# 32-head attention with its score operands in 48 partitions, two items' score products issued alternately

## What is computed

```python
q = layernorm(x)                       # (4, 256, 256): 32 heads of 8
k = v = ctx                            # (4, 256, 64):   8 heads of 8
# for each sequence b, group g, head h of the group:
scores = q[b, g, h] @ k[b, g].T * 8 ** -0.5      # 256 x 256
x[b, g, h] += softmax(scores) @ v[b, g]          # 256 x 8
```

## Time and profile before

| | |
|---|---|
| median of 3 runs | 812.61 us (811.94 to 814.03) |
| span of the profiled execution | 812.5 us |
| PE / DVE / ACT / POOL busy, whole span | 89% / 71% / 52% / 24% |
| the stage, first score product to last output | about 590 to 712 us |
| loop of 28 items at the full clock | 3.19 us an item |

### The profile page before, as it was taken

The page is one execution under the profiler, slowest core; times in us unless marked ns, Lnnn a source line. Parts: engine busy times, 40 slices in busy tenths (PEclk is TensorE's granted clock), DMA queues, the critical chain, the costliest instruction groups (busy, mean ns, idle before and its releaser), DMA issues. The chain is left out here.

```text
span 812.5 us, 13314 instructions
## 1 busy us (share of the span) xinstructions
PE 722.5 (89%) x4826; PEld 462.7 (57%) x4826; DVE 577.6 (71%) x1117; ACT 425.3 (52%) x888; POOL 198.0 (24%) x298
## 2 busy tenths in 40 slices
PE   5999989999999999999757469999589999879997
PEld 3555666666666666666533345666344444368886
DVE  5578678686767667686669854565668999665666
ACT  4557753544636364543649655455366676533332
POOL 2422010303123030303225314120121111352450
PEclk9999999999999999999979679999859999969999
DMA  4725422111202111110153006130010323403111
GB/s 120 194 60 158 148 70 69 48 45 34 76 7 72 30 49 36 42 43 1 27 135 75 9 8 191 45 80 2 21 41 21 81 59 90 120 2 106 54 50 52
DMA packets 49760, 52.24 MB, mean 64 GB/s; under 512 B 10116, under 2 KB 40388, under 8 KB 49588
## 3 DMA queue, kind: packets, MB, share of 16 engines
q1 hardware_dynamic: 49062, 51.06, 23.4%
q10 hardware_dynamic: 634, 0.33, 0.2%
HBM read 26.58 MB, written 2.04 MB: 35 GB/s over the span
## 5 line engine op out<-in xcount | busy, mean ns | idle before, releaser
L427 DVE TENSOR_REDUCE a_nm<-ps 128x2 f32<-128x512 f32 (+1 forms) x112 | 75.3, 688 | 28.4 <-PE ps L723 19.4
L2499 DVE TENSOR_REDUCE x_nm<-ps 128x2 f32<-128x512 f32 x128 | 84.9, 685 | 12.4 <-PE ps L2640 10.1
L2584 ACT ACTIVATE x_pt<-ps 128x1024 f32<-128x1024 f32 x64 | 62.4, 1020 | 34.6 <-PE ps L2668 33.9
L1535 PE MATMUL ps<-m_xp,m_mp 128*128 128x512 f32 x288 | 75.4, 397 | 1.0 <-DVE m_wr L1227 1.0
L1406 ACT ACTIVATE m_junk<-ps,m_nm 128x256 bf16<-128x256 f32 x128 | 58.6, 483 | 25.8 <-DVE m_nm L1244 25.8
L1191 POOL TENSOR_SCALAR fw<-fw,finv 128x256 f32<-128x256 f32 x24 | 11.6, 482 | 223.7 <-PE ps L1613 223.7
L2640 PE MATMUL ps<-kx,a_qs 96*128 96x256 bf16 x256 | 53.1, 296 | 8.2 <-DMA a_qs<-a_ks 6.5
L1535 PEld LDWEIGHTS ps<-m_xp,m_mp 128*128 128x128 f32 x288 | 50.7, 188 | 15.4 <-issue 6.1
L3068 PE MATMUL ps<-x_xp,x_wp 128*128 128x512 f32 x216 | 55.2, 407 | 0.0
L1207 DVE TENSOR_TENSOR m_qcs<-ps,mw_tab 64x512 f32<-64x512 f32 x64 | 44.0, 688 | 7.5 <-PE ps L1535 4.3
L1214 DVE TENSOR_TENSOR m_qcs<-ps,mw_tab 128x512 f32<-128x512 f32 x64 | 41.1, 684 | 7.4 <-PE ps L1535 7.1
(11 more groups left out here) (306 smaller groups left out, 1673.8 us busy)
## 6 DMA issues: line engine op xcount, KB each, us to landing
a_qs<-a_parts SPq DMA_DIRECT2D x48, 128.0 KB
a_ks<-a_parts SPq DMA_DIRECT2D x48, 128.0 KB
m_q<-m_qs SPq DMA_DIRECT2D x32, 128.0 KB
x_gb<-scr_g SPq DMA_DIRECT2D x8, 512.0 KB, 3.8
fw<-in_f_w SPq DMA_DIRECT2D x12, 256.0 KB
a_qs<-a_ks SPq DMA_DIRECT2D x48, 64.0 KB
mw_wq<-in_m_wq SPq DMA_DIRECT2D x8, 256.0 KB, 2.8
mw_wo<-in_m_wo SPq DMA_DIRECT2D x8, 256.0 KB, 2.8
```

Of the source, the lines that this page charges most:

```text
L427: dve.tensor_reduce(dst, src, AX.X, ALU.max, negate=True).then_inc(mx_done.sem, 1)
L1535: mm = pe.matmul(c.ps[:, QB_BANKS[k], :], mp[:, p % 2, w, dt, tile * P:(tile + 1) * P], xp[:, x, dt, half_cols(half)], start=((dt, w, x) = ...
L2499: dve.tensor_reduce(nm[:, n % ITEMS, QT * u:QT * u + QT], c.ps[:, u % 2, :].rearrange("p (t k) -> p t k", t=QT), AX.X, ALU.max, negate=Tru ...
L2584: act.activation(pt[:, n % 2, kt, :], c.ps[:, 2 + 2 * kt:4 + 2 * kt, :].rearrange("p b n -> p (b n)"), ACT.Exp, scale=SCALE).then_inc(exp_ ...
```

## The change

The zero rows are gone: S_ROWS is 48 and T_ROWS is 50. Items take turns at partitions 0 and 64 (even n at 0, odd n at 64), so that two items' operands lie in separate halves of the rows. The key tile is written twice, once for each half. A query transfer that read 128 partitions becomes two that read 64 each, one to each half; with the same memory the query tile holds six units and not three. `place` and the head layout of the normalised input are changed so that each half receives the right heads. On PE, each S of item n + 4 is issued around one T matmul of item n + 1: S first half, T matmul, S second half.

```diff
-    GROUPS, S_ROWS, T_ROWS, HD = 8, 96, 98, 8
+    GROUPS, S_ROWS, T_ROWS, HD = 8, 48, 50, 8
+    BASES = (0, 64)
...
-    def clear(self, sp):
-
-        sp.wait_ge(self.made.sem, 2)
-        some = slice(TERMS * self.HD, self.S_ROWS)
-        sp.dma_start(self.kx[some, :, :], self.zeros[some, :].unsqueeze(1)
-                     .broadcast_to([self.S_ROWS - TERMS * self.HD, self.GROUPS, TOK])).then_inc(self.sent.sem, 16)
...
     def send(self, sp):
+        for base in self.BASES:
+            sp.dma_start(self.kx[base + self.S_ROWS:base + self.T_ROWS, :, :],
+                         self.ones[0:2, :].unsqueeze(1).broadcast_to([2, self.GROUPS, TOK])).then_inc(self.sent.sem, 16)
...
-                    sp.dma_start(self.kx[term:TERMS * self.HD:TERMS, :, :], self.parts[:, part, :]).then_inc(self.sent.sem, 16)
-        sp.dma_start(self.kx[self.S_ROWS:self.T_ROWS, :, :],
-                     self.ones[0:2, :].unsqueeze(1).broadcast_to([2, self.GROUPS, TOK])).then_inc(self.sent.sem, 16)
-        sp.wait_ge(self.sent.sem, 16 * (TERMS + 2))
+                    for base in self.BASES:
+                        sp.dma_start(self.kx[base + term:base + self.S_ROWS:TERMS, :, :], self.parts[:, part, :])\
+                            .then_inc(self.sent.sem, 16)
+        sp.wait_ge(self.sent.sem, 16 * 2 * (TERMS + 1))
...
         def place(n):
 
-            return n // GROUPS, n % GROUPS
+            return n // GROUPS, n % GROUPS // 4 * 4 + (0, 2, 1, 3)[n % 4]
...
-        def queries(rows, n, h, count=1):
-            return qx[rows, n // 4 % RINGS, 4 * (n % 4) + h:4 * (n % 4) + h + count, :]
+        def own_rows(n, first, last):
+
+            return slice(BASES[n % 2] + first, BASES[n % 2] + last)
+
+        def queries(n, first, last, h, count=1):
+            at = n % 4 // 2 * 4 + h
+            return qx[own_rows(n, first, last), n // 4 % SLOTS_Q, at:at + count, :]
...
-                            sp.dma_start(qx[term:TERMS * HD:TERMS, k % RINGS, :, :], parts[:, dt, part, seq_cols(b)])\
-                                .then_inc(part_in[k].sem, 16)
+                            for s, base in enumerate(BASES):
+                                sp.dma_start(qx[base + term:base + S_ROWS:TERMS, k % SLOTS_Q, :, :],
+                                             parts[64 * s:64 * s + 64, dt, part, seq_cols(b)])\
+                                    .then_inc(part_in[k].sem, 16)
...
+                def side_by_side(n, u, n_t, kt, h):
+
+                    may_score(n, u)
+                    if h == 0:
+                        may_score_t(n_t, kt)
+                    score(n, u, 0)
+                    mm = score_t(n_t, kt, h)
+                    if h:
+                        mm.then_inc(st_done.sem, 1)
+                    score(n, u, 1).then_inc(s_done.sem, 1)
...
                 for n in range(N - LAG):
-                    scores(n + LAG, 0)
-                    scores_t(n + 1, 0)
-                    scores(n + LAG, 1)
+                    side_by_side(n + LAG, 0, n + 1, 0, 0)
+                    side_by_side(n + LAG, 1, n + 1, 0, 2)
                     product(n, 0)
                     max_transpose(n + TLAG)
-                    scores(n + LAG, 2)
+                    side_by_side(n + LAG, 2, n + 1, 1, 0)
                     product(n, 1)
-                    scores(n + LAG, 3)
-                    scores_t(n + 1, 1)
+                    side_by_side(n + LAG, 3, n + 1, 1, 2)
```

More of the change, by code:

```diff
@@ L1869, in _ @@
                         .then_inc(w_in, 16)
-                keys.clear(sp)
+                sp.wait_ge(keys.made.sem, 1)
                 alibi.moves(sp, keys)
@@ L2192, in open @@
         self.turnable = sb("ordered", [P, TT, CTX])
-        self.ones, self.zeros = sb("ones", [P, TOK], BF16), sb("zeros", [P, TOK], BF16)
+        self.ones = sb("ones", [P, TOK], BF16)
         self.full, self.rest, self.parts = sb("full", [CTX, TOK]), sb("rest", [CTX, TOK]), sb("parts", [CTX, 3, TOK], BF16)
@@ L2224, in constants @@
         pool.memset(self.ones[:, :], 1.0).then_inc(self.made.sem, 1)
-        pool.memset(self.zeros[:, :], 0.0).then_inc(self.made.sem, 1)
-    def clear(self, sp):
-        sp.wait_ge(self.made.sem, 2)
-        some = slice(TERMS * self.HD, self.S_ROWS)
-        sp.dma_start(self.kx[some, :, :], self.zeros[some, :].unsqueeze(1)
-                     .broadcast_to([self.S_ROWS - TERMS * self.HD, self.GROUPS, TOK])).then_inc(self.sent.sem, 16)
     def remainder(self, pool):
@@ L2265, in cross_attention @@
     N = BATCH * GROUPS
-    S_ROWS, T_ROWS = keys.S_ROWS, keys.T_ROWS
-    UNITS = N // 4
+    S_ROWS, T_ROWS, BASES = keys.S_ROWS, keys.T_ROWS, keys.BASES
+    UNITS, SLOTS_Q = N // 4, 2 * RINGS
+    SHARE = HEADS // 4
     LAG, TLAG = 4, 3
@@ L2296, in cross_attention @@
         dense = sb("dense", [DENSE_ROWS, BATCH - 1, 4, SEQ])
-        qx = c.qflat[:, :].rearrange("p (r h q) -> p r h q", r=RINGS, h=HEADS // 2)
+        qx = c.qflat[:, :].rearrange("p (r h q) -> p r h q", r=SLOTS_Q, h=SHARE)
         kx = keys.kx
@@ L2340, in head_inner @@
         def head_inner(t):
-            return c.xn[:, t, :].rearrange("p (a d h) -> p a h d", a=DT, d=HD)
+            return c.xn[:, t, :].rearrange("p (e d h) -> p e h d", d=HD, h=SHARE)
         def head_outer(t):
-            return c.x[:, t, :].rearrange("p (a h d) -> p a h d", a=DT, d=HD)
+            return c.x[:, t, :].rearrange("p (e h d) -> p e h d", d=HD, h=SHARE)
         def residual(s):
@@ L2369, in shift_rows @@
         def shift_rows(n):
-            return queries(slice(S_ROWS, T_ROWS), n, 0, 4)
+            return queries(n, S_ROWS, T_ROWS, 0, 4)
         with nc.Block() as block:
@@ L2416, in _ @@
                     if RINGS <= k < UNITS and step < 3:
-                        if step == 0:
-                            sp.wait_ge(st_done.sem, st_done.at(8 * (k - RINGS + 1)))
+                        if step == 0 and k >= SLOTS_Q:
+                            sp.wait_ge(st_done.sem, st_done.at(8 * (k - SLOTS_Q + 1)))
                         send(k, step, (hi_done, mid_done, lo_done)[step])
@@ L2629, in turn, with may_score, score, scores @@
                     mm.then_inc(xn_tr.sem, 1)
[L2631 to L2634, removed]
+                def may_score(n, u):
                     if u == 0 and n % 4 == 0:
-                        pe.wait_ge(part_in[n // 4].sem, part_in[n // 4].at(16 * TERMS))
+                        pe.wait_ge(part_in[n // 4].sem, part_in[n // 4].at(16 * 2 * TERMS))
                     if n > 0 or u > 1:
                         pe.wait_ge(mx_done.sem, mx_done.at(4 * n + u - 1))
[L2639 to L2643, removed]
+                def score(n, u, qt):
+                    b, g = place(n)
+                    return pe.matmul(c.ps[:, u % 2, qt * SEQ:(qt + 1) * SEQ],
+                                     queries(n, 0, S_ROWS, u).squeeze(1)[:, qt * P:(qt + 1) * P],
+                                     kx[own_rows(n, 0, S_ROWS), g, seq_cols(b)], start=True, stop=True)
+                def scores(n, u):
+                    may_score(n, u)
+                    score(n, u, 0)
+                    score(n, u, 1).then_inc(s_done.sem, 1)
                 def max_transpose(n):
@@ L2655, in max_transpose, with may_score_t @@
                     mm.then_inc(tr_done.sem, 1)
[L2657 to L2660, removed]
+                def may_score_t(n, kt):
                     if kt == 0:
@@ L2666, in scores_t, with score_t @@
                         pe.wait_ge(rest_done.sem, rest_done.at(2))
[L2667 to L2672, removed]
+                def score_t(n, kt, h):
+                    b, g = place(n)
+                    return pe.matmul(c.ps[:, 2 + 2 * kt + h // 2, :],
+                                     kx[own_rows(n, 0, T_ROWS), g, b * SEQ + kt * P:b * SEQ + (kt + 1) * P],
+                                     queries(n, 0, T_ROWS, h, 2).rearrange("p h q -> p (h q)"), start=True, stop=True)
+                def scores_t(n, kt):
+                    if n >= N:
+                        return
+                    may_score_t(n, kt)
+                    score_t(n, kt, 0)
+                    score_t(n, kt, 2).then_inc(st_done.sem, 1)
+                def side_by_side(n, u, n_t, kt, h):
+                    may_score(n, u)
+                    if h == 0:
+                        may_score_t(n_t, kt)
+                    score(n, u, 0)
+                    mm = score_t(n_t, kt, h)
+                    if h:
+                        mm.then_inc(st_done.sem, 1)
+                    score(n, u, 1).then_inc(s_done.sem, 1)
                 def product(n, kt):
@@ L2765, in cross_attention @@
         for s in part_in:
-            s.done(16 * TERMS)
+            s.done(16 * 2 * TERMS)
         for s in m_in:
```

## The result

The changed kernel takes 822.38 us (821.83 to 823.24, 4 runs) against 813.31 us for the kernel before: a ratio of 1.0112, 95% interval 1.0098 to 1.0127. It is slower by 9 us. The prediction said slower, but with 864 us: the likeliest case did not happen. Each ratio here leaves out runs more than 1.5% above the kernel's fastest, which are two of the four of e7 (836.28 and 839.07 us) and one of the twelve of e11 (2025.92 us), while the medians are of all runs.

The account below looks back on a forecast made before the run. The prediction took the loop to be bound by PE's own order, with DVE right behind. With PE's clock staying at 0.50 it summed 812.5 + 3.9 (start) + 39.8 (loop) + 7.8 (tail) = 864.0 us, stated range 812 to 868.

Parts of the forecast that it names:

- the likeliest case: PE's clock stays at 0.50 through the 32-head stage's loop: loop +39.8 us, tail +7.8, 864 us in all; chance 0.42.
- the two signs that the prediction gave for being wrong: Clock depends on how steadily PE works, not on rows used; or the denser stretch around the two products suffices.
- The overlap: In the loop both row halves work at once, taking T off PE's queue: 3.04 us an item at 1.00, 0.15 less.
- Rival D: Row halves don't overlap in the loop: 830 us at clock 1.00, 899 at 0.50; chance 0.07.
- The start: First score product waits for twelve query transfers, not six, at 0.66 us each: +3.9 us, bounds +0.8 to +4.4.
- rival C: Clock rises and half-size transfers issue at 0.40 us: loop gains 3.9 us, start costs 0.8, 809.4 us; chance 0.07.
- SP's queue: Six sends delay the next row of maxima; after two result rows it is late, twice: +1.6 us at 1.00, 0 at 0.50.
- my own ring of 3.04: The loop's chain R3, S1, P0, S2, P1, S3, R3 as next bound: 3.04 us an item at 1.00, 4.72 at 0.50.
- The tail: Last four items at clock 0.50 cost 1.7 us more each, plus 1 for the end: +7.8 us, uncertain by 4.
- rival A: Clock rises with the loop's first products, as before: items of 3.04 us, 815 us (811 to 819); chance 0.26.
- The key tile: Seven more issues, 4.8 us, hidden by 16 us of cover on SP before its next issue: 0.
- B: Clock rises late, after 5 to 20 loop items at 0.50 costing 1.7 us each: 822 to 850 us; chance 0.18.

Follow-up runs that it names:

- e7: The changed kernel, both row halves in use, but with PE's old order (S pair, T pair): median 832.70 us, ratio 1.0130 to the kernel before.
- e11: The kernel before with 14 extra matmuls of 128 rows, result unread, ahead of its first score product: 813.04 us, ratio 0.9997.
- e3: The kernel before with 48 and 50 rows for 96 and 98, all items at partition 0, old order, no zero rows: 891.64 us, ratio 1.0977.
- e9: e6 with a few extra matmuls of 128 rows and 512 columns, result unread, in gaps of the tail: 814.80 us, ratio 1.0013 to the kernel before.
- e8: The kernel before with 48 and 50 rows, all items at partition 0, and PE's new order S, T, S: 896.58 us, ratio 1.101.
- e6: e5 with query unit 0 sent lower half first, so item 0 waits for six transfers only: 814.56 us, ratio 1.0019 to the kernel before.
- e5: e1 with two query transfers sent ahead of the loop and four, not three, in its first two items: 816.74 us, ratio 1.0040 to the kernel before.
- e1: The changed kernel with query transfers dealt out over the items, mostly three each, instead of six, four, two, none: 822.27 us, ratio 1.0104 to the kernel before.

## Why the prediction was wrong, point by point

**The step that failed** is the clock: "I take as likeliest that it stays at 0.50 through the loop." It rose at 613.9, after the first item, and the +39.8 us for the loop and +7.8 for the tail, which hang on it, came out as +3.75 and +0.4. What was right in it: rows count (e3 stayed at 0.50 from 606 to 772 with 48 and 50 rows, where the same order with 96 and 98 rows rose to 1.00 at 610.6), and the price of an item at 0.50 (4.72 us predicted; 4.72 in e9, 4.68 in e7; DVE's maxima take 0.69 us at 0.50 as at 1.00, at 642.08 in e8 and at 629.83 before). For the prologue the measured part is this: granted 0.50 from 590 to 607 with 96 and 98 rows, PE busy 14.62 of 17.00 us, and 0.50 from 590 to 606 with 48 and 50 rows, PE busy 11.74 of 16.00 us. In e11, with the rows of before, it was granted 0.50 from 591.6 to 608.5 at 14.98 of 16.90 us busy, though 1.00 just ahead. That such work is "not enough for 1.00" is my reading of this. What was wrong: that the clock would not rise with two 48-row products side by side and pauses between them. With overlap the clock rose in every profile, at once or some items late; without overlap (e3, e8) it stayed at 0.50 through the loop. All kernels with overlap also use both halves of the rows, and none without it does, so which of the two counts is not shown. Of the two signs that the prediction gave for being wrong, the second, that the stretch around the two products suffices, fits the changed kernel; the same products did not suffice in e3. The first, that steadiness counts and not rows, fails in e3: PE was busy for 166.00 of 166.00 us, at 0.50, and in the changed kernel for 26.71 of 34.10 us, at 1.00. Nor does my theory of rows separate the cases by itself. How much work a rise takes was not measured; that it comes at once in e6 (609.2) and three items late in e9 (623.6), whose programs are the same up to the tail, suggests that this loop has little to spare. All four runs of the changed kernel itself lie within 1.4 us.

**The overlap** was right. Predicted 3.04 us an item at 1.00, measured 3.09, before 3.19; R3 to P0 takes 1.08 us for 1.06 and S3 to R3 0.46 for 0.43, the rest is as predicted. That the two row halves work at once, on which the 3.04 and the 4.72 rest, no row before the change showed; it was an assumption. The run after shows it: S and T start together at 643.68, and P1 follows at 644.00, as it did 0.32 us after S2 alone (638.06 to 638.38 before). Two S matmuls of 256 columns do take as long as one T of 512: before, S to T is 0.22 us (636.43 to 636.65) and two T 0.44 (636.65 to 637.09). Rival D is out.

**The start** was right: +3.9 predicted, +3.5 measured, and e6 takes it away. The bound of +0.8 and with it rival C are out, since a half-size transfer costs the same 0.66 us of issue.

**SP's queue** was the right mechanism with the wrong size: +1.6 us predicted, +6.4 measured, some 3.9 of it late rows and 2.5 the clock. I had counted two late rows and let each be late by itself. I had also set the queue's 24.2 us against eight items of the old length, 25.4 us, though my own ring of 3.04 gave 24.3. In fact the queue had almost no slack left (24.2 of 24.7 us for eight items at 3.09), so that a delay lived on through the items behind it; four sends took 3.12 us where I had 2.6; and after a pause of 2.2 us the clock fell, with which two items went from 3.09 to 5.77 and 4.50. In e5, without such a pause, it stays at 1.00 through the loop.

**The tail** is 0.4 us longer at the same clock, where the sum of rival A had nothing (the last section has its place). **The key tile** was indeed free: its fourteen issues end at 453.4 and SP's next one is at 474.75, and the first transfer of queries goes out at 583.88 against 583.77.

With the clock as it was, the sum has the form of rival A's with each term as measured: 812.5 + 3.5 - 2.7 + 6.4 + 0.4 + 0.3 = 820.4, the span of 820.5; A had +3.9, -3.9, +1.6 and +1 for a late rise, 815. That 822.4 us lies in the stated range of 812 to 868 is owed to the width of the range, which covers A and B, not to the likeliest case.

## What to carry to other kernels

A gain of 0.1 us an item on one engine was paid for with twice the issues on a queue that feeds it: count issues against the time of one item, and look at what small urgent transfer stands behind the large ones. Deal transfers out evenly, with each deadline worked out, before judging the idea that needs them. And where PE's clock is at 0.50 before a loop, fewer rows in the matmuls can keep it there (e3: for the 166 us from 606 to 772). Here it rose again, at 613.9, with two products side by side, but with little margin: with the waits of 2.2 us (changed kernel, clock down from 648) and 3.7 us (e1, down from 675.6) came a fall of the clock, and they cost more than their length; with one of 1.6 us, at 675.41 in the changed kernel, none came; in e7, where less overlaps, one came with a wait of 1.2 us.

## What the runs showed of the hardware that was not expected

- Zero rows are not idle rows for the clock: with 96 rows of which 48 are zero it rose at 610.6, with the same work in 48 rows it stayed at 0.50 through the loop, and the kernel took 891.64 us against 812.63.
- The turn of 72 rows starts later behind a T over a row half. In the tail it starts 0.53 us after T; before the change, with T over 98 rows, 0.44 us. The changed kernel's timeline:

```profile
709.27 0.60 PE L2674 MATMUL ps<-a_qs,kx 50*128 50x512 bf16 x2
...
709.80 0.72 PE L2721 MATMUL ps<-ident,x_dense 72*128 72x72 f32 x8
```

The same two groups on the timeline of the kernel before:

```profile
701.87 0.60 PE L2668 MATMUL ps<-a_qs,kx 98*128 98x512 bf16 x2
...
702.31 0.67 PE L2699 MATMUL ps<-ident,x_dense 72*128 72x72 f32 x8
```

The difference is 0.09 us; its cause is not shown. The load of the turn's stationary operand starts at 709.80, with the turn, and before the change at 702.10, during T. The P behind the turn comes 0.05 us later too, 0.65 us for 0.60, and this 0.14 us at three places is the tail's +0.4. From S to P, also from a half to full rows, no such delay shows: 0.32 us with either kernel (643.68 to 644.00 after, 638.06 to 638.38 before).
- Issue time on SP's queue was the same, 0.66 us, for transfers of 64 KB and of 32 KB between the same tiles, and 0.66 for the 4 KB row of maxima; the read of 288 KB of results took 0.31.
